# A quarter's even columns moved ahead of the softmax's exponential on ScalarE (graph attention with a sparse mask, then routed experts)

## The chip, the cores and the metric

One core of one Trainium2 chip. The metric is the device time of one launch in microseconds (us); lower is better. The kernel before takes 1185.52 us, the median of three runs (1185.07 to 1197.87).

## What is computed

```python
# x: 8192 x 256 f32; adj: 8192 x 8192 int32, about 1 in 2048 entries is 1, the others 0
h  = layernorm(x);  Wh = h @ W
e  = (Wh @ a1)[:, None] + (Wh @ a2)[None, :];  e = where(e > 0, e, 0.2 * e)
e  = where(adj > 0, e, -9e15)
x  = x + elu(softmax(e, axis=1) @ Wh)
h  = layernorm(x);  idx = argmax(h @ router_w.T + router_b)        # one of 32 experts
x  = x + relu(relu(h @ W1[idx] + b1[idx]) @ W2[idx] + b2[idx])
```

The mask `adj` is 268 MB, and reading it is most of the traffic. A row has about four neighbours, so the attention works on lists of neighbours and not on the full matrix.

## The kernel before

The 8192 rows are 64 strips of 128 rows. The program is written engine by engine, each engine with its own queue of instructions in the order of the code, and with counting semaphores between them. It has three stages: a table of `Wh` rows is built (eight groups of eight strips), then come the rounds, one step `u` for each strip, and then the experts work through blocks of tokens. The change lies in the rounds. A step handles several strips at once:

- **ScalarE** (`step` under `@block.scalar`) turns the mask of strip u+5 from int32 into fp8 bytes. A strip has four quarters of 2048 columns. The function `signs` (L711) writes one quarter with two instructions: the even columns (L717, ACT.Identity, out `sg`) and the odd columns (L719, ACT.Sign, out `sg`). The second one counts the semaphore `a_sg`. In a step the order is: `attention_sum` (L733, out `hh`), `count_tail` (L756, L758), quarter 0, `transposes2` (L744), quarter 1, `softmax_exp` (L749, out `pr` and `den`), `elu_exp` (L738, out `ex`), quarter 2, quarter 3.
- **SyncE** (queue SPq) loads the mask in halves of 2 MB (L427, `raw_all<-in_adj`). There are three half buffers. A load waits at L426 for `a_sg`, that is until ScalarE has finished the half that lies in its buffer. So each step issues two loads: one behind quarter 1 (here called load A) and one behind quarter 3 (load B).
- **TensorE** folds the bytes of a strip into words (`fold`, L1512 and L1514, out `psF`), and computes the weighted sum of the gathered rows (L1577, L1579), the tail's small products (L1546 to L1569) and fillers (L1503) that keep it busy.
- **VectorE** finds the neighbours in the words (L891 to L957), and does the softmax's scores (L1086 to L1106), the elu and the second normalisation (L1128 to L1158), and the place of each token with its expert (L1163 to L1196). It has by far the most instructions in a step, and works through them strictly in order.
- **GpSimd** issues the indirect DMAs on a queue of its own: at first the scatter of strip u-2 (L633, `regions<-x,posu`), then six gathers for strip u+1 (L611, `G_all<-wh_table,idx`): one for each of the first five neighbours, and a sixth, the tail gather, for all the neighbours beyond them, packed into slots.

Two of VectorE's instructions wait for those DMAs: L1086 (`slot_s`) for all six gathers of the strip, and L1140 (`x<-el,x_sb`) for the scatter that reads its buffer `x1`, of which there are two.

The rounds have 64 full steps, of which 59 read the mask ahead; most of these run in a loop whose body is two steps on most engines and six on ScalarE and SyncE.

Of the kernel before, what the change touches and what calls it, by code (L numbers as in the profile page):

```python
# [27 lines left out]
TINY = 1.0e-20  # L28
# [8 lines left out]
def gat_moe(nc, x, adj, gW, ga, rw, rb, W1, b1, W2, b2, out, table, region):  # L37
    f32, i32, u32 = mybir.dt.float32, mybir.dt.int32, mybir.dt.uint32
    bf16, f8 = mybir.dt.bfloat16, mybir.dt.float8e4
    ALU, ACT, AX = mybir.AluOpType, mybir.ActivationFunctionType, mybir.AxisListType  # L40
# [4 lines left out]
    LAG = NG // 2  # L45
# [15 lines left out]
    with ctx:  # L61
        def sb(name, shape, dt=f32):
            return ctx.enter_context(nc.sbuf_tensor(name, shape, dt))
# [4 lines left out]
        def sem(name):  # L68
            return ctx.enter_context(nc.semaphore(name))
# [22 lines left out]
        minus_half = sb("minus_half", [P, GROUP])  # L92
        minus_tiny = sb("minus_tiny", [P, 1])
# [35 lines left out]
        sign_of = [[[sg[i][:, q, :].bitcast(f8).rearrange("p (w b) -> p b w", b=2)[:, b, :] for b in range(2)] for q in range(Q)] for i in range(2)]  # L129
        raw_of = [[[raw[n][k].rearrange("p (w b) -> p b w", b=2)[:, b, :] for b in range(2)] for k in range(2)] for n in range(THIRDS)]  # L130
# [129 lines left out]
        a_sg = sem("a_sg")  # L260
# [104 lines left out]
        def half_place(strip, h):  # L365


            turn, rest = strip
            n = 2 * rest + h
            return n % THIRDS, turn * 2 + n // THIRDS  # L370
# [320 lines left out]
        def _(act):  # L691
# [16 lines left out]
                act.nop(nofuse=True)  # L708
                act.activation(xT[r % 2][:, :, :].rearrange("p h n -> p (h n)"), psXn[r % 2][:, 0:D], ACT.Copy).then_inc(a_xT, 1)  # L709

            def signs(t, par, q, strip):  # L711

                b, count = half_place(strip, q // 2)
                act.wait_ge(raw_in[b], count * 16 + 16)
                act.wait_ge(pe_fold, t * 2 + q // 2 + 1)
                act.nop(nofuse=True)
                act.activation(sign_of[par][q][0], raw_of[b][q % 2][0], ACT.Identity, bias=minus_tiny[:, 0:1], scale=TINY,  # L717
                               saturate=False)
                act.activation(sign_of[par][q][1], raw_of[b][q % 2][1], ACT.Sign, bias=minus_half[:, 0:1],  # L719
                               saturate=False).then_inc(a_sg, 1)  # L720

            def group(g, par, i, behind, ahead):
                for r in range(GROUP):
                    transposes(g * GROUP + r, r)
                    if r % 4 == 2:
                        signs(i, i % 2, 2 * par + r // 4, divmod(i, THIRDS))
            groups(act, group)

            def attention_sum(w, par):

                act.wait_ge(pe_o, w + 3)
                act.wait_ge(v_post, w * VP + VP + 2)
                act.activation(hh[:, :], psO[par][:, 0:D], ACT.Copy, scale=rden[par][:, 0:1]).then_inc(a_h, 1)  # L733

            def elu_exp(w):

                act.wait_ge(v_post, w * VP + 2 * VP + 1)
                act.activation(ex[:, :], um[:, :], ACT.Exp).then_inc(a_ex, 1)  # L738

            def transposes2(w):  # L740

                act.wait_ge(pe_t2, w + 1)
                act.wait_ge(pe_lg, w + 1)
                act.activation(xT2[:, :, :].rearrange("p h n -> p (h n)"), psT[:, 0:D], ACT.Copy).then_inc(a_x2, 1)  # L744

            def softmax_exp(u):

                act.wait_ge(v_sm, u * VS + VS)
                act.activation(pr[:, :], ee[:, :], ACT.Exp, bias=nmx[:, 0:1], accum_out=den[:, 0:1]).then_inc(a_p, 1)  # L749

            def count_tail(u, par):

                act.wait_ge(pe_slot, u + 1)
                act.wait_ge(v_dec, u * VD + VD)
                with nc.allow_low_precision(reason="counts of at most 11 are exact"):
                    act.activation(tail_sign[par][:, :], keys[:, bass.ds(u, 1), KD:K].rearrange("p o k -> p (o k)"), ACT.Sign,  # L756
                                   accum_out=tails[:, bass.ds(u, 1)]).then_inc(a_tail, 1)
                act.activation(tail_row[par][:, 0:KT], keys[:, bass.ds(u, 1), KD:K].rearrange("p o k -> p (o k)"),  # L758
                               ACT.Copy).then_inc(a_tail, 1)
# [3 lines left out]
            for q in range(Q):  # L763
                signs(LAG, 0, q, divmod(LAG, THIRDS))

            def step(u, par, do, strip):
                if do.post:
                    attention_sum(u - 1, 1 - par)
                if do.prepare:
                    count_tail(u + 2, par)  # L770
                if do.ahead:
                    signs(u + LAG + 1, 1 - par, 0, strip)
                if do.place:
                    transposes2(u - 2)
                if do.ahead:
                    signs(u + LAG + 1, 1 - par, 1, strip)
                if do.attend:
                    softmax_exp(u)
                if do.post:
                    elu_exp(u - 1)  # L780
                if do.ahead:
                    signs(u + LAG + 1, 1 - par, 2, strip)
                    signs(u + LAG + 1, 1 - par, 3, strip)
            rounds_of_six(act, step)

            act.wait_ge(v_flag, 6)
# [944 lines left out]
```

## Time and profile before

| | |
|---|---|
| median of three runs | 1185.52 us (1185.07 to 1197.87) |
| the profiled execution: its own time, its span | 1188.4 us, 1186.6 us |
| busy over the span (page): VectorE, ScalarE, TensorE, GpSimd | 894.5, 795.4, 900.9, 656.9 us |
| the rounds that this text counts in, from the scatter at 207.70 us to that at 935.58 us | 54 steps, 727.88 us |
| moved over the span | 357.33 MB, mean 301 GB/s |

The span is the time from the first to the last instruction. "Busy" counts the instructions of an engine that ran; a wait is shown as the idle time ahead of an instruction, with what ended it. For DMAs the profile tells when the instruction that issues one ran, and how long after it the data had landed.

### The profile page before, as it was taken

The page shows a single profiled execution, that of the slowest core. Times are in us where ns is not written, and L with a number is a line of the kernel's source. Part 1 is how long each engine was busy: PE and PEld are TensorE (multiplying, and loading weights), DVE is VectorE, ACT ScalarE, POOL GpSimd, SP SyncE. Part 2 cuts the span into 40 slices and gives each one's busy share as a digit, 9 for nine tenths or more (in the row PEclk, how much of TensorE's full clock was granted, in tenths as well). Part 3 has the DMA queues.
Part 4 walks back from the last instruction along what each step waited for, and adds up shares of the span by engine and source line. Part 5 has one row for each costly group of instructions (what it writes and reads, how often), then busy time and mean ns, then how long its engine had stood idle before and what let it go on. Part 6 is the DMA issues. An engine that isn't in the chain of part 4 may idle for free.

```text
span 1186.6 us, 25008 instructions
## 1 busy us (share of the span) xinstructions
PE 900.9 (76%) x4388; PEld 560.6 (47%) x4389; DVE 894.5 (75%) x4327; ACT 795.4 (67%) x1339; POOL 656.9 (55%) x700
## 2 busy tenths in 40 slices
PE   2777728788878888688887878878888875558995
PEld 1545515444444444354454444445445444446774
DVE  5788727688888878788888878878888876555563
ACT  0444549688887878688788877878878831136663
POOL 3555545556656655555565556655566556326664
PEclk9999959899999989899999999989999986679998
DMA  6677788899999999899999989998999995035651
GB/s 227 219 270 266 295 335 345 318 376 377 376 371 368 362 349 365 330 341 381 363 381 349 368 323 371 366 361 336 374 381 383 341 251 129 29 105 162 173 170 60
DMA packets 84715, 357.33 MB, mean 301 GB/s; under 512 B 26006, under 2 KB 52591, under 8 KB 68289
## 3 DMA queue, kind: packets, MB, share of 16 engines
q1 hardware_dynamic: 56226, 296.78, 67.7%
q0 software_dynamic: 27712, 60.06, 14.7%
q8 instruction: 12, 0.20, 0.1%
q14 instruction: 29, 0.24, 0.1%
q10 hardware_dynamic: 736, 0.05, 0.0%
HBM read 343.67 MB, written 32.05 MB: 317 GB/s over the span
## 4 chain that ended last, share of the span: by engine, by line
DVE 29%; DMA 23%; issue 22%; PE 13%; POOL 7%; DVEq 2%; ACT 2%; POOLq 0%; ACTq 0%
DMA regions<-x,posu 13%; DMA G_all<-wh_table,idx 7%; POOL G_all L611 4%; PE psO L1704 2%; DVE top_word L891 2%; PE psW L1494 2%; PE psO L1577 2%; POOL out_x L673 2%; DVE xn L1158 1%; DVE begun L1058 1%; DVE lidx L1173 1%; PE psO L1503 1%; DVE oh L1181 1%; DVE xn L985 1%; DVE el L1132 1%
## 5 line engine op out<-in xcount | busy, mean ns | idle before, releaser
L611 POOL DMA_INDIRECT G_all<-wh_table,idx x384 | 398.7, 1038 | 136.4 <-issue 128.7
L717 ACT ACTIVATE sg<-raw_all,minus_tiny 128x1024 fp8e4<-128x1024 int32 x256 | 311.8, 1218 | 0.1
L719 ACT ACTIVATE sg<-raw_all,minus_half 128x1024 fp8e4<-128x1024 int32 x256 | 311.1, 1215 | 0.0
L1503 PE MATMUL psO<-word_no,share 128*128 128x512 bf16 x885 | 244.0, 411 | 0.0
L633 POOL DMA_INDIRECT regions<-x,posu x64 | 67.4, 1053 | 213.9 <-DVE idx L1050 115.7
L1577 PE MATMUL psO<-G_all,diag 128*128 128x256 f32 x640 | 163.2, 405 | 22.9 <-DVE diag L1115 22.9
L1577 PEld LDWEIGHTS psO<-G_all,diag 128*128 128x128 f32 x640 | 124.3, 201 | 64.9 <-issue 48.4
L1512 PE MATMUL psF<-sg,fold_w 128*128 128x512 bf16 x512 | 136.0, 389 | 7.3 <-DVE top_word L891 2.7
L1503 PEld LDWEIGHTS psO<-word_no,share 128*128 128x128 bf16 x885 | 93.6, 111 | 92.9 <-issue 26.8
L749 ACT ACTIVATE pr<-ee,nmx 128x16 f32<-128x16 f32 x64 | 19.7, 307 | 146.3 <-DVE nmx L1106 146.3
L673 POOL DMA_INDIRECT out_x<-raw_all,tok x81 | 78.9, 974 | 56.6 <-issue 29.9
L891 DVE MAX8 top_word<-psF 128x8 f32<-128x256 f32 x256 | 103.0, 425 | 6.7 <-PE psF L1514 0.5
L1494 PE MATMUL psW<-w_aug,xT 128*128 128x258 f32 x256 | 69.5, 395 | 13.8 <-ACT xT L709 13.8
L583 POOL TENSOR_TENSOR xn_sum<-xn_sum,xn 128x256 f32<-128x256 f32 x64 | 47.5, 742 | 40.7 <-DVE xn L985 39.8
L1512 PEld LDWEIGHTS psF<-sg,fold_w 128*128 128x128 bf16 x512 | 47.1, 108 | 43.8 <-issue 13.4
L1704 PE MATMUL psO<-x_sb,hT 128*128 x162 | 56.0, 428 | 8.9 <-ACT hT L825 3.7
L1563 PE MATMUL psW<-slot_s,to_row 128*128 128x11 f32 x128 | 22.3, 248 | 49.3 <-DVE slot_s L1086 49.1
L627 POOL TENSOR_TENSOR x<-ve,minus_half 128x1 f32<-128x1 f32 x64 | 36.8, 576 | 35.6 <-DVE x L1154 34.7
L1563 PEld LDWEIGHTS psW<-slot_s,to_row 128*128 128x128 f32 x128 | 22.8, 204 | 69.8 <-issue 68.7
L1494 PEld LDWEIGHTS psW<-w_aug,xT 128*128 128x128 f32 x256 | 44.8, 195 | 22.7 <-issue 18.9
L817 ACT ACTIVATE w_b<-x_sb 128x129 f32 x84 | 26.3, 313 | 43.0 <-ACT hT L825 30.2
L1086 DVE TENSOR_SCALAR slot_s<-slot_col,G_all 128x11 f32<-128x11 f32 x64 | 16.6, 260 | 47.9 <-DMA G_all<-wh_table,idx 46.9
(217 smaller groups left out, 1837.5 us busy)
## 6 DMA issues: line engine op xcount, KB each, us to landing
raw_all<-in_adj SPq DMA_DIRECT2D x128, 2048.0 KB, 10.0
raw_all<-regions SPq DMA_DIRECT2D x84, 130.0 KB, 2.2
wh_table<-G_all POOLq DMA_DIRECT2D x8, 1040.0 KB, 10.0
x_sb<-in_x SPq DMA_DIRECT2D x8, 1024.0 KB, 5.7
G_all<-wh_table,idx POOLq DMA_INDIRECT x384, 6.1
regions<-pad_row SPq DMA_DIRECT2D x32, 130.0 KB
x_sb<-in_L_ffn_W SPq DMA_DIRECT2D x4, 512.0 KB
x_sb<-in_L_ffn_W SPq DMA_DIRECT2D x8, 256.0 KB
```

The costliest lines, as they stand in the source:

```text
L583: pool.tensor_tensor(xn_sum[:, :], xn_sum[:, :], xn[r % 2][:, :], ALU.add).then_inc(pl_sum, 1)
L611: pool.indirect_dma_start(out=G[par][:, k, :], out_offset=None, in_=table[:, :], in_offset=bass.IndirectOffsetOnAxis(ap=idx[par][:, k:k + ...
L633: pool.indirect_dma_start(out=region[:, :], out_offset=bass.IndirectOffsetOnAxis(ap=posu[par][:, 0:1], axis=0), in_=x1[par][:, :], in_offs ...
L673: pool.indirect_dma_start(out=out[:, :], out_offset=bass.IndirectOffsetOnAxis(ap=tok[r % STORES][:, 0:1], axis=0), in_=yb[r % STORES][:, : ...
L717: act.activation(sign_of[par][q][0], raw_of[b][q % 2][0], ACT.Identity, bias=minus_tiny[:, 0:1], scale=TINY, saturate=False)
L719: act.activation(sign_of[par][q][1], raw_of[b][q % 2][1], ACT.Sign, bias=minus_half[:, 0:1], saturate=False).then_inc(a_sg, 1)
L891: v.max(top_word[:, q, :], psF[q // 2][:, q % 2 * WORDS:(q % 2 + 1) * WORDS]).then_inc(v_top, 1)
L1494: mm = pe.matmul(psW[r % 2][:, 0:D + 2], xT[r % 2][:, h, :], w_aug[:, h, :], start=(h == 0), stop=(h == DH - 1))
L1503: pe.matmul(psO[par][:, :], share[:, :], word_no[:, 0:2, :].rearrange("p q w -> p (q w)"), start=True, stop=True)
L1512: pe.matmul(words, fold_w[:, j, :], sg[par][:, 2 * h:2 * h + 2, j * WORDS:(j + 1) * WORDS], start=(j == 0), stop=False)
L1577: pe.matmul(psO[par][:, 0:D], diag[:, k, :], G[par][:, k, 0:D], start=(k == 0), stop=False)
L1704: pe.matmul(psO[r % 2][:, 0:D], hT[r % 2][:, :], w2_sb[:, bass.ds(e, 1), :].rearrange("p o n -> p (o n)"), start=True, stop=True).then_inc ...
```

## The change

`signs` gets an argument that says which of the two byte columns it writes. In the step, quarter 2 is split: its even columns are written ahead of `softmax_exp`, its odd columns where the whole quarter was, behind `elu_exp`. Everything else stays.

```diff
-            def signs(t, par, q, strip):
+            def signs(t, par, q, strip, bytes=range(2)):
 
                 b, count = half_place(strip, q // 2)
                 act.wait_ge(raw_in[b], count * 16 + 16)
                 act.wait_ge(pe_fold, t * 2 + q // 2 + 1)
                 act.nop(nofuse=True)
-                act.activation(sign_of[par][q][0], raw_of[b][q % 2][0], ACT.Identity, bias=minus_tiny[:, 0:1], scale=TINY,
-                               saturate=False)
-                act.activation(sign_of[par][q][1], raw_of[b][q % 2][1], ACT.Sign, bias=minus_half[:, 0:1],
-                               saturate=False).then_inc(a_sg, 1)
+                if 0 in bytes:
+                    act.activation(sign_of[par][q][0], raw_of[b][q % 2][0], ACT.Identity, bias=minus_tiny[:, 0:1], scale=TINY,
+                                   saturate=False)
+                if 1 in bytes:
+                    act.activation(sign_of[par][q][1], raw_of[b][q % 2][1], ACT.Sign, bias=minus_half[:, 0:1],
+                                   saturate=False).then_inc(a_sg, 1)
...
                 if do.ahead:
                     signs(u + LAG + 1, 1 - par, 1, strip)
+                    signs(u + LAG + 1, 1 - par, 2, strip, range(1))
                 if do.attend:
                     softmax_exp(u)
                 if do.post:
                     elu_exp(u - 1)
                 if do.ahead:
-                    signs(u + LAG + 1, 1 - par, 2, strip)
+                    signs(u + LAG + 1, 1 - par, 2, strip, range(1, 2))
                     signs(u + LAG + 1, 1 - par, 3, strip)
```

ScalarE's queue in one step of the rounds, before, from the second instruction of quarter 1 to the first of the next step (in the names, `pr` is the softmax's exponential and `ex` the elu's):

```order
L719 ACTIVATE sg<-raw_all,minus_half 128x1024
L749 ACTIVATE pr,den<-ee,nmx 128x16
L738 ACTIVATE ex<-um 128x256
L717 ACTIVATE sg<-raw_all,minus_tiny 128x1024
L719 ACTIVATE sg<-raw_all,minus_half 128x1024
L717 ACTIVATE sg<-raw_all,minus_tiny 128x1024
L719 ACTIVATE sg<-raw_all,minus_half 128x1024
L733 ACTIVATE hh<-psO,rden 128x256
```

And after:

```order
L721 ACTIVATE sg<-raw_all,minus_half 128x1024
L718 ACTIVATE sg<-raw_all,minus_tiny 128x1024
L751 ACTIVATE pr,den<-ee,nmx 128x16
L740 ACTIVATE ex<-um 128x256
L721 ACTIVATE sg<-raw_all,minus_half 128x1024
L718 ACTIVATE sg<-raw_all,minus_tiny 128x1024
L721 ACTIVATE sg<-raw_all,minus_half 128x1024
L735 ACTIVATE hh<-psO,rden 128x256
```

One L717 (in the new file L718) has gone from behind `ex` to ahead of `pr`; the count of instructions is the same, and no other engine's order changes.

## Rows read from the trace of the kernel before

**Rows 1.** Rounds: window, us; busy PE, PEld, DVE, ACT, POOL; clock, DMA share, GB/s
```profile
207.70:935.58 727.88, 593.00 (x2864) 344.24 (x2862) 608.31 (x3132) 582.49 (x865) 423.44 (x432) 0.96 0.95 361
```

**Rows 2.** Waits of VectorE, 207 to 936 us: total, times, longest
```profile
DVE slot_s L1086 <- DMA G_all<-wh_table,idx: 23.3, 9, 4.7
DVE x L1140 <- DMA regions<-x,posu: 20.6, 23, 1.6
```

**Rows 3.** Timeline of GpSimd, two steps without such waits: start, duration [idle before]
```profile
884.64 1.06 POOL L633 DMA_INDIRECT regions<-x,posu  x1 [3.20 <-DVE idx L1050]
...
892.61 1.01 POOL L611 DMA_INDIRECT G_all<-wh_table,idx  x1 [0.30 <-DVE x L1154]
...
897.14 1.05 POOL L633 DMA_INDIRECT regions<-x,posu  x1 [2.90 <-DVE posu L1196]
...
910.11 1.06 POOL L633 DMA_INDIRECT regions<-x,posu  x1 [3.21 <-DVE idx L1050]
```

**Rows 4.** Timeline of ScalarE in two neighbouring steps
```profile
604.44 0.31 ACT L749 ACTIVATE pr<-ee,nmx 128x16 f32<-128x16 f32 x1 [1.98 <-DVE nmx L1106]
...
614.25 1.20 ACT L719 ACTIVATE sg<-raw_all,minus_half 128x1024 fp8e4<-128x1024 int32 x1
616.82 0.31 ACT L749 ACTIVATE pr<-ee,nmx 128x16 f32<-128x16 f32 x1 [1.37 <-DVE nmx L1106]
...
617.93 1.23 ACT L717 ACTIVATE sg<-raw_all,minus_tiny 128x1024 fp8e4<-128x1024 int32 x1
619.05 1.23 ACT L719 ACTIVATE sg<-raw_all,minus_half 128x1024 fp8e4<-128x1024 int32 x1
```

**Rows 5.** Source view of L749, 208 to 936 us: ScalarE's idle time before it
```profile
  DVE nmx L1106: 111.5, 54
```

**Rows 6.** Timeline of SyncE's loads (x2: from the first's start to the second's end)
```profile
602.67 7.98 SPq L427 DMA_DIRECT2D raw_all<-in_adj  x2
...
615.67 0.33 SPq L427 DMA_DIRECT2D raw_all<-in_adj  x1
...
622.75 7.00 SPq L427 DMA_DIRECT2D raw_all<-in_adj  x2
```

**Rows 7.** Timeline of VectorE: the instruction that needs the gathers, in two steps
```profile
613.96 0.23 DVE L1086 TENSOR_SCALAR slot_s<-slot_col,G_all 128x11 f32<-128x11 f32 x1
...
897.87 0.30 DVE L1086 TENSOR_SCALAR slot_s<-slot_col,G_all 128x11 f32<-128x11 f32 x1
```

**Rows 8.** Source view of L611, windows 608.9:609.2 and 621.7:622 (one tail gather each)
```profile
DMA to landing us min/median/max: 3.9/3.9/3.9
...
DMA to landing us min/median/max: 4.9/4.9/4.9
```

**Rows 9.** Timeline of SyncE: four other stretches with loads
```profile
181.21 6.18 SPq L427 DMA_DIRECT2D raw_all<-in_adj  x2
...
192.16 5.69 SPq L427 DMA_DIRECT2D raw_all<-in_adj  x2
...
216.18 7.32 SPq L427 DMA_DIRECT2D raw_all<-in_adj  x2
...
785.60 6.72 SPq L427 DMA_DIRECT2D raw_all<-in_adj  x2
```

**Rows 10.** L611, windows 187.6:189.7, 197.3:200.3, 216.1:216.4, 785.8:786.1 (the last two tail gathers)
```profile
L611 POOL DMA_INDIRECT G_all<-wh_table,idx x2: 1001/1256/1511, 187.7 to 189.5; - x2
DMA to landing us min/median/max: 6.3/6.7/7.2
...
L611 POOL DMA_INDIRECT G_all<-wh_table,idx x3: 1006/1027/1215, 197.4 to 200.1; - x3
DMA to landing us min/median/max: 7.6/7.7/8.3
...
DMA to landing us min/median/max: 9.9/9.9/9.9
...
DMA to landing us min/median/max: 8.7/8.7/8.7
```

## The prediction

> **What bounds the kernel now.** I read the busy table of the rounds first [rows 1]: of 727.88 us VectorE is busy 608, ScalarE 582, TensorE 593, and the DMA engines stand at a share of 0.95 with 361 GB/s. No compute engine is full, the DMA engines nearly are. The window holds 54 steps (as many exponentials in rows 5), so one takes 13.48 us, a pair 26.96.
>
> Then the waits of VectorE, which has 58 instructions a step and takes them strictly in order [rows 2]: 23.3 us for gathers ahead of `slot_s` (9 times, up to 4.7) and 20.6 us for the scatter ahead of L1140 (23 times). Together 43.9 us. Neither ScalarE nor TensorE takes more than a trace of VectorE's time. The scatters show what a pair costs without those waits: 910.11 - 884.64 = 25.47 us [rows 3]. Against 26.96 that is 1.49 more a pair, for 27 pairs 40 us, which agrees with the waits. So the step is VectorE's own queue (12.7 us) plus what it waits for small DMAs, and these wait because 4 MB of mask stream through the same 16 DMA engines in each step.
>
> Third, the timeline of ScalarE [rows 4]: it idles ahead of the softmax's exponential for 1.98 us in one step and 1.37 in the next, and that is so throughout: 111.5 us over 54 steps, 2.06 each [rows 5]. This idle time costs nothing in itself, since VectorE's `nmx` ends it.
>
> **The change, part by part.** *The moved instruction.* An L717 advances ScalarE's queue by 1.12 us (619.05 - 617.93) and is moved into the idle time. It can start where quarter 1 ends, at about 614.25 + 1.20 = 615.45, and lasts to some 616.65; the exponential starts at 616.82. So it fits with 0.2 us to spare in the tighter of two neighbouring steps and with 0.8 in the other [rows 4]. Cost on the exponential: nothing; bound above, 1.12 us in a step without idle time; the mean of 2.06 says that there are few. It adds a wait for the second half of the strip (load A of the step before) and for TensorE's fold, now ahead of the exponential, with `pr` and everything behind it queued. Load A is issued when quarter 1 ends and would be needed when quarter 1 ends again, one whole step later, 12.5 us or more. None of the `sg` instructions of rows 4 waited for a load. Cost nothing again, and that cover is one step long; if it were gone, each us that a load is late would be one of the step.
>
> *What comes earlier.* Behind `elu_exp` three instructions stand where four stood, so quarter 3 ends 1.12 us earlier, and `a_sg` lets SyncE issue load B 1.12 us earlier. ScalarE's next work (`hh`, `tail_sign`) waits for TensorE and VectorE soon anyway, so load A moves by 0 to 0.5 us. VectorE waits for nothing of this, so ScalarE's gain as such is worth 0.
>
> *What load B meets.* This is the term that decides. GpSimd's six gathers do not move: they follow the scatter. In one step the tail gather starts at about 609.0 and load B at 602.67 + 7.98 - 0.33 = 610.32, 1.3 us later; in the next the gather at 621.7 and load B at 622.75, one us later [rows 6, 8]. These two land 3.9 and 4.9 us after their start [rows 8]. VectorE needs them 5.0 us after it (613.96 - 608.96) in the one kind of step and 5.26 (897.87 - 892.61) in the other, when nothing else is late [rows 3, 7]. The slack is thus 0.4 to 1.1 us. After the change load B is issued 0.2 us behind the tail gather in the first kind and 0.1 ahead of it in the second.
>
> The trace has gathers that a load precedes or meets. Load at 187.06 (181.21 + 6.18 - 0.33): gathers at 187.7 and 189.5 land in 7.2 and 6.3 us. Load at 197.52: gathers from 197.4 to 200.1 in 7.6 to 8.3. Load at 216.18 and tail gather at 216.2: 9.9 us. Load at 785.60, tail gather at 785.9: 8.7 [rows 9, 10]. The mean of these seven (6.3, 7.2, 7.6, 7.7, 8.3, 8.7, 9.9) is 7.96. The last two stand at the very distance that the change makes, and VectorE's longest wait, 4.7 us [rows 2], is about what the 9.9 us leave (9.9 - 5.26 = 4.6). The ends are 6.3 and 9.9. I take the mean, since in the first two stretches the rounds were only starting, and in the last two GpSimd itself ran late in its step. The wait at `slot_s` is then 7.96 - 5.26 = 2.7 us; ends 1.04 and 4.64.
>
> It does not come in every step. A wait of w delays the exponential, hence load B, by w, while that step's own gathers have already been issued; the load is then 1 us or more behind the tail gather and this one lands in time. So every second step. A pair takes 25.47 + 2.7 = 28.2 us, with the scatter's waits gone: behind a late `slot_s` VectorE reaches L1140 late, and load B landing 1.1 us sooner frees the scatter in the other. Against 26.96 that is +1.2, for 27 pairs +33 us. Ends: 26.5 us and -12 us; 30.1 us and +85 us. Below the lower end only VectorE's waits are left to gain.
>
> The Trainium skill (page "DMA: Bandwidth & Descriptors", section "Queues, rings and completion order") says that each DMA engine alternates between the rings for which it has work, and changes only after a whole packet, typically some 9 to 17 descriptors; and that a completion is written only after all earlier writes of that DMA engine, of whatever queue. By that rule a gather behind a load waits for a large part of the load's share, and lands about when the load does. The trace agrees in kind (9.9 and 8.7 us, against 3.9 and 4.9).
>
> **Sum.** The profiled execution took 1188.4 us, its span 1186.6, so 1.8 us lie around it. 1188.4 + 33 = 1221; the median of the runs shown is 2.9 us lower, at 1185.5, so 1185.5 + 33 = 1219 us.
>
> **Rivals.** *A, faster: the scatter gains and the tail gather doesn't lose.* Load B lands 1.1 us sooner, so the scatter ahead of L1140 meets less of it, and the 20.6 us go [rows 2]. For it: in 23 of 54 steps that wait is there, at most 1.6 us, about what the load moves by. If `slot_s` goes on costing its 23.3, or a little more, that gives -15 to -20, some 1168 us. Against it [rows 9, 10]: no gather beside or behind a load's issue landed under 6.3 us. *B, no difference:* the two DMA effects cancel (w near 1.5 gives 26.97 a pair, exactly the pair of now), or VectorE's own queue sets all. 1185.5 us. For it: the DMA engines move the same bytes in both, and nobody waits for ScalarE. *C, much slower: the tail gather always lands with load B.* Then w is 4.64, a pair 30.1, +85 us, 1271. It decides from the point where load B's issue comes less than about 0.3 us behind the tail gather's in all steps. For it the two tail gathers of rows 10, 8.7 and 9.9; against it the lighter traffic that a longer pair brings, which lets a load land sooner. This is what the rule of the Trainium skill cited above (same page and section) gives if it holds in every such step. *D, the change fills nothing:* the exponential is late by the moved instruction. It costs at most 1.12 us a step, +60, 1246. Against it the idle times [rows 4, 5].
>
> **Chances.** The forecast (w between 1.9 and 4, 1196 to 1253 us) 0.40; C 0.13; D 0.02; B 0.20; A 0.25. A measurement of this kernel tells about 1% from no change. Faster by over 1%: 0.25; within 1%: 0.20; slower by over 1%: 0.55. For 8 in 10 the range takes in A's value at the low end and C's at the high end: 1168 to 1271.
>
> **What would show it.** Right: `slot_s` L1086 waits for `G_all` in some 25 of 54 steps, 2 to 4 us each, over 60 us in total; L1140's wait for the scatter falls under 10 us; the tail gathers before those waits land in 7 us or more; load B is issued within 0.3 us of the tail gather in the steps of 12.5 us; ScalarE's idle time ahead of `pr` alternates between about 0.5 and 3 us. Wrong: a pair of 26 us or less, with L1140 and `slot_s` both under their 20.6 and 23.3 us; then an early load does not hold up a gather, and its landing hangs on something else, as on GpSimd being late. Wrong in another way if load B is not issued earlier at all, because ScalarE waits for `um` or for the mask.

## The result, and the profile after

The changed kernel takes 1208.81 us, the median of four runs (1204.37 to 1212.42), against 1185.39 (1185.07 to 1197.87): a ratio of 1.0227, 95% interval 1.0169 to 1.0286. It is slower by 1.7 to 2.9%, as forecast (1219). The profiled execution took 1208.17 us, its span 1206.4; the one of before took 1188.4 and 1186.6, 3 us above its median. So the two traces have 19.8 us to explain.

The first view is the window that answers to [rows 1]: the same 54 steps of the rounds, now from the scatter at 210.39 us to that at 952.01 us. The columns are those of [rows 1].

```profile
210.39:952.01 741.62, 585.68 (x2810) 347.50 (x2862) 607.26 (x3132) 588.12 (x865) 424.41 (x433) 0.96 0.93 354
```

VectorE has its 3132 instructions and 607 us of work as before; ScalarE its 865. Only the time around them grew: 741.62 against 727.88, or 13.7 us. The rest lies outside the window: 2.7 us ahead of it (210.39 - 207.70) and 3.4 behind it (1206.4 - 952.01 against 1186.6 - 935.58; there the waits at `slot_s` went from 3.7 to 6.3 us). 2.7 + 13.7 + 3.4 = 19.8.

The waits of VectorE in that window, which answer to [rows 2]:

```profile
DVE slot_s L1089 <- DMA G_all<-wh_table,idx: 59.3, 27, 5.1
DVE idx L1053 <- issue: 13.2, 27, 0.6
DVE xn L1161 <- POOL x L627: 0.3, 1, 0.3
```

L1089 is the old L1086. It waits 27 times in 54 steps, 2.2 us each, where it waited 9 times for 23.3 us together. The wait of 20.6 us for the scatter is gone from the list altogether. So one wait took the place of the other, and more: 59.3 - 23.3 - 20.6 = +15.4 us, near the 13.7 by which the window grew.

Here are two neighbouring steps. First ScalarE, as in [rows 4]; L718 is now the even half of a quarter and L721 the odd one:

```profile
612.60 1.19 ACT L721 ACTIVATE sg<-raw_all,minus_half 128x1024 fp8e4<-128x1024 int32 x1
613.69 1.20 ACT L718 ACTIVATE sg<-raw_all,minus_tiny 128x1024 fp8e4<-128x1024 int32 x1
615.54 0.31 ACT L751 ACTIVATE pr<-ee,nmx 128x16 f32<-128x16 f32 x1 [0.65 <-DVE nmx L1109]
...
616.28 0.42 ACT L740 ACTIVATE ex<-um 128x256 f32<-128x256 f32 x1 [0.34 <-DVE um L1131]
...
618.84 1.22 ACT L721 ACTIVATE sg<-raw_all,minus_half 128x1024 fp8e4<-128x1024 int32 x1
620.67 0.47 ACT L735 ACTIVATE hh<-psO,rden 128x256 f32<-128x256 f32 x1 [0.60 <-PE psO L1582]
```

The moved instruction (613.69) sits in the idle time, and 0.65 us of that are left; `pr` is not late. Quarter 3 ends at 620.06 (618.84 + 1.22), one instruction earlier than it would behind the old order. What that frees is idle time again, ahead of `hh`. Now the issues, SyncE's loads (an issue of x2 spans both) and GpSimd's scatters (L633) and tail gathers:

```profile
614.01 6.62 SPq L427 DMA_DIRECT2D raw_all<-in_adj  x2
...
626.76 8.19 SPq L427 DMA_DIRECT2D raw_all<-in_adj  x2
```

```profile
611.91 1.05 POOL L633 DMA_INDIRECT regions<-x,posu  x1 [3.63 <-DVE posu L1199]
...
620.07 1.01 POOL L611 DMA_INDIRECT G_all<-wh_table,idx  x1 [0.30 <-issue]
...
624.88 1.06 POOL L633 DMA_INDIRECT regions<-x,posu  x1 [3.20 <-DVE idx L1053]
...
633.08 1.02 POOL L611 DMA_INDIRECT G_all<-wh_table,idx  x1 [0.31 <-issue]
```

And VectorE's instruction that needs the gathers:

```profile
627.11 0.23 DVE L1089 TENSOR_SCALAR slot_s<-slot_col,G_all 128x11 f32<-128x11 f32 x1 [1.97 <-DMA G_all<-wh_table,idx]
...
639.75 0.30 DVE L1089 TENSOR_SCALAR slot_s<-slot_col,G_all 128x11 f32<-128x11 f32 x1
...
653.95 0.41 DVE L1089 TENSOR_SCALAR slot_s<-slot_col,G_all 128x11 f32<-128x11 f32 x1 [1.71 <-DMA G_all<-wh_table,idx]
```

Load B goes out at 614.01 + 6.62 - 0.33 = 620.30 (0.33 is the length of one issue), 0.2 us behind the tail gather at 620.07. VectorE gets that gather's data 7.0 us after its start and has waited 1.97 us. The wait pushes the next exponential and with it the next load B to 626.76 + 8.19 - 0.33 = 634.62, 1.5 us behind the tail gather at 633.08; there is no wait at 639.75. In the step after, it is back. Over the middle of the rounds (300 to 700 us, 29 tail gathers) load B stands either 0.1 ahead to 0.3 us behind the tail gather, or 1.5 to 2.7 behind (5.6 once), about half and half; before, it stood 1.0 or 1.35 behind in most steps.

### The profile page after: what moved, and what is told of

Same layout as the page of the kernel before. It is cut to its first block, busy times and chain, and to the rows that moved or that the text cites. A ratio compares the mean times of both kernels' runs of the same rounds, so it can differ in the third digit from the quotient of the medians.

```text
span 1206.4 us, 25000 instructions
## 1 busy us (share of the span) xinstructions
PE 896.2 (74%) x4321; PEld 567.2 (47%) x4389; DVE 893.5 (74%) x4327; ACT 801.1 (66%) x1339; POOL 657.4 (54%) x700
## 4 chain that ended last, share of the span: by engine, by line
DVE 26%; issue 23%; DMA 22%; PE 13%; POOL 9%; ACT 3%; DVEq 2%; POOLq 0%; ACTq 0%; another core or an unknown queue 0%
DMA G_all<-wh_table,idx 17%; POOL G_all L611 7%; PE psO L1707 3%; DMA regions<-x,posu 2%; PE psO L1580 2%; DVE top_word L894 2%; PE psW L1497 2%; DVE el L1135 1%; POOL out_x L673 1%; PE psL L1696 1%; DVE xn L988 1%; ACT sg L721 1%; ACT sg L718 1%; DMA out_x<-raw_all,tok 1%; DVE xn L1161 1%
## 5 line engine op out<-in xcount | busy, mean ns | idle before, releaser
L611 POOL DMA_INDIRECT G_all<-wh_table,idx x384 | 399.4, 1040 | 136.9 <-issue 127.5
L718 ACT ACTIVATE sg<-raw_all,minus_tiny 128x1024 fp8e4<-128x1024 int32 x256 | 311.8, 1218 | 1.9 <-DMA raw_all<-in_adj 1.8
L721 ACT ACTIVATE sg<-raw_all,minus_half 128x1024 fp8e4<-128x1024 int32 x256 | 311.2, 1216 | 0.0
L1506 PE MATMUL psO<-word_no,share 128*128 128x512 bf16 x827 | 229.6, 410 | 3.2 <-issue 0.2
L633 POOL DMA_INDIRECT regions<-x,posu x64 | 67.5, 1054 | 215.4 <-DVE idx L1053 117.9
L1580 PEld LDWEIGHTS psO<-G_all,diag 128*128 128x128 f32 x640 | 129.0, 207 | 60.9 <-issue 43.2
L1506 PEld LDWEIGHTS psO<-word_no,share 128*128 128x128 bf16 x885 | 92.5, 109 | 87.1 <-issue 17.1
L735 ACT ACTIVATE hh<-psO,rden 128x256 f32<-128x256 f32 x64 | 30.4, 475 | 77.6 <-PE psO L1582 77.6
L1089 DVE TENSOR_SCALAR slot_s<-slot_col,G_all 128x11 f32<-128x11 f32 x64 | 16.3, 255 | 84.1 <-DMA G_all<-wh_table,idx 83.6
L1515 PEld LDWEIGHTS psF<-sg,fold_w 128*128 128x128 bf16 x512 | 47.2, 108 | 44.8 <-issue 13.8
```

What stands on the lines that cost most here:

```text
L611: pool.indirect_dma_start(out=G[par][:, k, :], out_offset=None, in_=table[:, :], in_offset=bass.IndirectOffsetOnAxis(ap=idx[par][:, k:k + ...
L633: pool.indirect_dma_start(out=region[:, :], out_offset=bass.IndirectOffsetOnAxis(ap=posu[par][:, 0:1], axis=0), in_=x1[par][:, :], in_offs ...
L1506: pe.matmul(psO[par][:, :], share[:, :], word_no[:, 0:2, :].rearrange("p q w -> p (q w)"), start=True, stop=True)
L1515: pe.matmul(words, fold_w[:, j, :], sg[par][:, 2 * h:2 * h + 2, j * WORDS:(j + 1) * WORDS], start=(j == 0), stop=False)
L1580: pe.matmul(psO[par][:, 0:D], diag[:, k, :], G[par][:, k, 0:D], start=(k == 0), stop=False)
```

## The experiments

Each ratio is against the kernel before, timed beside the run. "Gathers" is VectorE's total wait for gathers and "scatter" that for the scatter, both between 207 and 936 us of the profiled execution. That execution can be some 0.7% off the median of its kernel, so its waits go with its own time and not with the ratio. The code shown leaves out the `nop` behind each wait and the argument `late`, which is set for the loads in the rounds' steps.

### Load B late again, the new order kept

```diff
...
+                if late and h == 0:
+                    sp.wait_ge(a_tail, 2 * t - 7)
...
```

SyncE waits for one count more ahead of load B; nothing else differs from the changed kernel.

> The changed kernel, but SyncE's load B waits also for ScalarE's tail_sign behind quarter 3, so it is issued about 1 us later, where it was before the change; ScalarE's order stays the changed one. Theory 1 (an early load B holds up the tail gather): the waits at slot_s fall from over 80 us to 20-30 us, the scatter's waits return to some 20 us, 1180 to 1192 us. Rival (the new order on ScalarE costs by itself, by the added wait ahead of the exponential or by where the bytes come): it stays at 1203 to 1212 us, slot_s over 60 us.

Ratio 0.9997 (0.9961 to 1.0034), 1182.45 us. Load B now stands 1.67 us behind the tail gather (median of 30). VectorE's waits:

```profile
DVE x L1146 <- DMA regions<-x,posu: 26.0, 29, 2.6
DVE idx L1056 <- issue: 13.2, 27, 0.6
DVE slot_s L1092 <- DMA G_all<-wh_table,idx: 1.4, 4, 0.5
```

One wait on SyncE's queue, which does no work, takes back the whole 2%. So the new order on ScalarE costs nothing in itself that these runs can tell: its cost is the moment of load B. The gathers fell further than expected (1.4 us for 20 to 30), as this wait puts load B a little later than it was before the change, and the profiled execution (1173.99 us) was the fastest of ten.

### The same delay on the kernel before

> The kernel before, with the same added wait ahead of load B: issued about 1 us later than before, some 2 us behind the tail gather. Theory 1: the rare long landings of the tail gather (9 to 11 us) go, slot_s waits under 10 us; the scatter may wait longer since the load lands later (20 to 45 us), so 1165 to 1195 us. Rival: 1185 +- 4 us, slot_s as before at 23 us in the rounds.

Ratio 0.9966 (0.9934 to 0.9998), 1179.74 us; load B 1.9 us behind the tail gather.

```profile
DVE x L1143 <- DMA regions<-x,posu: 26.0, 36, 1.9
...
DVE slot_s L1089 <- DMA G_all<-wh_table,idx: 6.6, 4, 3.2
```

The gathers' waits went from 23.3 to 6.6 us as expected, the scatter's rose to 26.0. The gain is a third of a per cent and hardly clear of the measurement. Against the run above only the order on ScalarE differs, and the two intervals overlap.

### Load B much later

```diff
...
+                if late and h == 0:
+                    sp.wait_ge(a_sg, t * Q + 1)
...
```

> The changed kernel, load B waits also for quarter 0 of the next strip: some 3.5 us later than in the changed kernel. Theory 1: slot_s waits under 10 us, as the tail gather has landed when the load starts; but the load is then used less than 10 us after its issue, or the scatter meets more of it, so waits of ScalarE for the mask or of L1140 for the scatter come up: 1180 to 1215 us. Rival (order by itself): 1205 us or more with slot_s still over 60 us.

Ratio 1.0324 (1.0286 to 1.0362), 1221.36 us, a little above the range given, with load B 5.1 us behind the tail gather. No wait for gathers is in the list; it begins with

```profile
DVE x L1146 <- DMA regions<-x,posu: 72.3, 52, 2.6
```

ScalarE never waited for the mask in the rounds. Both theories allowed a slow result here, but with different waits, and the gathers' are gone. The load has an enemy on either side: too early it meets the tail gather, too late the scatter. One caution: the tail gather itself takes 5.4 us here (median of 26 landings), more than the 5.0 us at which VectorE asked for it before. That is not seen as a wait, as VectorE, held up by the scatter, mostly comes to `slot_s` only 6 us or more after that gather's start.

### Load B between

```diff
...
+                if late and h == 0:
+                    sp.wait_ge(a_h, t - 4)
...
```

> Dose between the changed kernel and the first run: load B waits for hh (ScalarE's instruction right behind quarter 3, itself waiting for TensorE), which puts it 0.4 to 0.9 us later than in the changed kernel. Theory 1: the waits at slot_s lie between 59 us (changed kernel) and 1.4 us (the run with about 1 us), say 5 to 35, and the scatter's between 0 and 26; 1180 to 1200 us. Rival (any wait on SyncE's queue would do): as the first run.

Ratio 0.9956 (0.9912 to 1.0000), 1180.51 us. `hh` itself waits for TensorE, so load B stands 1.3 us behind the tail gather, later than I had meant.

```profile
DVE x L1146 <- DMA regions<-x,posu: 16.6, 23, 2.8
DVE slot_s L1092 <- DMA G_all<-wh_table,idx: 13.8, 10, 3.4
```

These runs and the two kernels give a curve, all with two buffers and the tail gather last (the median distance is taken between 300 and 700 us):

| load B behind the tail gather (median), us | order on ScalarE | gathers, us | scatter, us | profiled execution, us | ratio of the medians |
|---|---|---|---|---|---|
| 0.3 (alternating -0.1..0.3 and 1.5..2.7) | new | 59.3 | 0 | 1208.17 | 1.0227 |
| 1.3 | old | 23.3 | 20.6 | 1188.4 | 1 |
| 1.3 | new | 13.8 | 16.6 | 1176.39 | 0.9956 |
| 1.7 | new | 1.4 | 26.0 | 1173.99 | 0.9997 |
| 1.9 | old | 6.6 | 26.0 | 1177.82 | 0.9966 |
| 5.1 | new | 0 | 72.3 | 1220.96 | 1.0324 |

At like distance both orders cost alike to within half a per cent, and the bottom is flat between 1.3 and 1.9 us. The two kinds of wait account for nearly all of the rest: taken off the profiled time they leave 1144.5 to 1148.9 us in all six rows, while the waits themselves go from 27.4 to 72.3 us.

### The tail gather first

```diff
-                gather(par, KD, GATHERS, gat)
+                gather(par, KD, GATHERS, gat_t)
...
-                    gather(1 - par, 0, KD, gat)
                     gather_tail(u + 1, 1 - par)
+                    gather(1 - par, 0, KD, gat)
...
-                v.wait_ge(gat[par], i16)
+                v.wait_ge(gat_t[par], i16)
...
+                v.wait_ge(gat[par], half_up(u, par) * KD)
```

`slot_s` needs only the tail gather; the other five are needed by the softmax's first instruction, 2.1 us later. With the new order:

> The changed kernel, GpSimd issues the tail gather first of the six and with a semaphore of its own; slot_s waits for that alone, the softmax's first instruction (about 2 us later) for the other five. Load B as early as in the changed kernel. Theory 1: slot_s does not wait for gathers any more; the fifth gather is now the last one, beside load B, but needed 2.1 us later, so of the waits of 2 us nearly nothing is left; the scatter's waits stay away as in the changed kernel: a pair of 25.5 to 26.2 us, 1145 to 1170 us. Rival (order by itself): 1200 us or more.

Ratio 1.0070 (1.0046 to 1.0094), 1192.42 us: better than the changed kernel, and not what I expected.

```profile
DVE sc L1102 <- DMA G_all<-wh_table,idx: 36.8, 29, 3.5
...
DVE x L1145 <- DMA regions<-x,posu: 1.0, 4, 0.3
```

`slot_s` no longer waits, but the softmax does in 29 of the steps, 1.27 us on average, though it comes 2.1 us later. In these 29 steps the gather that is now last is there about 2.1 + 1.27 - 2.2 = 1.2 us later after its start than the tail gather was. I had assumed the two alike. In ten more steps load B stood as near and nothing waited. The number of rows hardly explains it: with one entry in 2048, I estimate 48 rows of a strip with a fifth neighbour and 53 neighbours beyond the fifth. Why it takes longer stays open.

The same on the old order:

> Old order on ScalarE, tail gather first with a semaphore of its own. Load B is issued 1 us or more behind the last gather, which now has 2.1 us more until it is needed. Theory 1: the gathers' waits fall from 23.3 us to under 12 (what is left of the landings of 9 to 11 us), the scatter's waits stay at 20 to 28 us or grow by what is gained: 1172 to 1184 us. Rival (the gathers' waits are not bound to which gather is the last): 1185 us.

Ratio 0.9904 (0.9869 to 0.9940), 1174.24 us.

```profile
DVE sc L1099 <- DMA G_all<-wh_table,idx: 20.0, 12, 3.6
DVE x L1142 <- DMA regions<-x,posu: 19.4, 25, 1.6
```

The time came as expected, the waits did not: 20.0 us for gathers and not under 12. This profiled execution (1181.37 us) was among the slower of its ten, so part of the gain is not in it.

The two steps together, with the new order and load B behind `hh`:

> Changed order, tail gather first, load B behind hh. With the last gather needed 2.1 us later and load B 0.4 to 0.9 us later than in the changed kernel, theory 1 has the gathers' waits fall from 36.8 us (the same with load B early) to 5 to 20 and the scatter's stay under 15: 1168 to 1184 us, better than both kernels. Rival (a fixed sum: what one DMA gains the other loses): 1185 to 1192 us.

Ratio 0.9880 (0.9830 to 0.9929), 1169.00 us: the lowest of all, 1.2% below the kernel before (0.7 to 1.7%), though its interval overlaps with that of the last run. The profiled execution was its fastest of seven (1161.32 us).

```profile
DVE x L1148 <- DMA regions<-x,posu: 17.0, 22, 1.6
DVE idx L1057 <- issue: 13.2, 27, 0.6
DVE sc L1105 <- DMA G_all<-wh_table,idx: 4.4, 3, 1.8
```

And with load B behind `tail_sign`:

> As the last, load B behind tail_sign, about 1 us later than in the changed kernel. Gathers' waits under 5 us, the scatter's 20 to 28 us as in the first run: 1176 to 1186 us.

Ratio 0.9899 (0.9854 to 0.9943), 1174.29 us; it can't be told from the last two. Gathers 4.3 us, scatter 30.6, a little more than expected.

### Three buffers for the scatter

If the scatter's waits and the gathers' are all that stands above VectorE's own queue, a third buffer `x1` (with one more for the places, `posu`) removes the first kind. It needs loop bodies of six steps on VectorE and GpSimd, so a control has those alone:

```diff
...
-            rounds(pool, step)
+            rounds_of_six(pool, step)
...
-            rounds(v, step)
+            rounds_of_six(v, step)
```

> Control for the next three: the kernel before with VectorE's and GpSimd's loop bodies six steps long instead of two, nothing else. The loop's turn costs VectorE 0.5 us ahead of the first instruction of every second step (13.2 us in the rounds of the kernel before); that should fall to about 4.5 us. Where that idle time covers the scatter's landing, it comes back as a wait at L1140. Expected 1176 to 1187 us; a wait on fetched code could make it slower.

Ratio 1.0406 (1.0311 to 1.0501), 1243.18 us. The control alone is 4% slower, which I had given as a mere possibility.

```profile
DVE idx L1050 <- issue: 50.2, 9, 7.0
DVE slot_s L1086 <- DMA G_all<-wh_table,idx: 32.2, 18, 5.1
DVE x L1140 <- DMA regions<-x,posu: 22.1, 18, 2.8
```

The turn of the loop now comes 9 times and costs 5.6 us each, for 27 times 0.49. Three more instructions of VectorE idle without a releaser, 12.4 us together, where the kernel before has 0.2. These two and the gathers' 8.9 us more add up to 58 of the 59 us between the two profiled spans. The page of the profile counts 97 packets on the queue for instructions where the kernel before has 29:

```profile
q14 instruction: 97, 0.79, 0.2%
```

The three-buffer kernels are read against this control only:

```diff
...
-        x1 = [sb(f"x1{i}", [P, ROW]) for i in range(2)]
+        x1 = [sb(f"x1{i}", [P, ROW]) for i in range(3)]
...
-                    scatter(u - 2, par)
+                    scatter(u - 2, par, (strip[1] + 2) % 3, sc_out)
...
-                    post_x1(w, 1 - par, x_rows(w), None if isinstance(w, int) and w < 2 else half_done(w, 1 - par))
+                    post_x1(w, strip[1], x_rows(w), None if isinstance(w, int) and w < 3 else strip[0] * 16 - 32)
```

> As the control, and three buffers x1 instead of two, so that VectorE waits for the scatter of three strips ago. If the rounds are VectorE's queue plus the waits for the scatter and for the tail gather, the waits at L1140 (20 to 26 us) go to zero and the time falls by 12 to 25 us against the control, unless the gained time comes back at slot_s: with shorter steps the DMA engines are fuller and load B still meets the tail gather within 1 us. 1155 to 1175 us. If the DMA engines' throughput bounds the rounds instead, it is within 5 us of the control and the waits move to slot_s.

1228.14 us (1224 to 1244), 15 less than the control (1235 to 1249), within the 12 to 25 expected of the difference; the absolute time was missed with the control's. The scatter's wait is gone, the gathers' the same:

```profile
DVE slot_s L1090 <- DMA G_all<-wh_table,idx: 31.7, 26, 6.3
```

With the new order:

> As the last, with the changed order on ScalarE. Theory 1 (an early load B holds up the tail gather): the waits at slot_s stay at some 2 us in every second step, 45 to 60 us together, since no scatter is involved; the time is 1190 to 1205 us, 20 us or more above the same kernel with the old order. Rival (the scatter's buffers are what the early load disturbs): the difference between the two orders goes.

1253.87 us (1245 to 1257), 25.7 more than the same with the old order (+2.1%, as large as the change's own effect). The difference came as expected, the absolute time did not; the waits are fewer and longer, 3.5 us in 17 steps:

```profile
DVE slot_s L1093 <- DMA G_all<-wh_table,idx: 59.2, 17, 6.5
```

No scatter waits in either, so what the early load costs does not go by way of the scatter's buffers.

Old order, load B behind the next quarter 0:

> Three buffers x1, old order on ScalarE, and load B issued only behind quarter 0 of the next strip, some 2.4 us later than before. Theory 1: the late load costs only at the scatter (as in the third run of the first set), which no longer matters, and leaves the tail gather free: both waits near zero, a pair of steps 25.5 us less the loop's turn, 1140 to 1155 us. If instead the load is now late for ScalarE (it is used about 11 us after its issue and lands in 10), waits of sg for the mask appear and it is 1155 to 1185 us.

1218.92 us, 24 less than the control, but the gathers' waits did not vanish: 43.7 us in 34 steps, more than the control's 32.2. Most of the 24 us is not a gain of the DMAs either: the loop's turns cost 32.1 us here and 50.2 in the control, for a reason that no run shows. The two loads are now issued 2.5 us apart, around the scatter, and the gathers follow right behind them:

```profile
607.65 2.82 SPq L431 DMA_DIRECT2D raw_all<-in_adj  x2
```

```profile
608.12 1.06 POOL L636 DMA_INDIRECT regions<-x,posu  x1 [3.64 <-DVE idx L1057]
```

I had counted only the distance of load B to the tail gather ahead of it, and not that a load too late is a load ahead of the next step's gathers. (That these two loads are what holds them up is argued from the timeline; this trace has no landings of the gathers. In the run with load B much later, where the two loads stand alike, the tail gather takes 5.4 us.)

## Why the prediction was right, and where it was off

**The moved instruction costs nothing.** Right in the window: 0.65 us of idle time are left ahead of `pr` in the step shown, and over the window ScalarE still idles there 87.1 us, where it was 111.5. In five of the 54 steps no idle time was left, yet VectorE waited for `pr` in none of them. Its bound, "there are few" steps without idle time, was true and not nothing. In two of the three steps ahead of the window VectorE waited for `pr`; in the kernel before, its waits of this kind came to 0.5 us in the whole run:

```profile
188.22 0.16 DVE L1114 RECIPROCAL rden<-den 128x1 f32<-128x1 f32 x1 [0.83 <-ACT pr L751]
...
200.82 0.16 DVE L1114 RECIPROCAL rden<-den 128x1 f32<-128x1 f32 x1 [1.11 <-ACT pr L751]
```

That is 1.9 us in the stretch that grew by 2.7: rival D, in two steps of 64. Other waits of VectorE moved both ways there (1.9 us less for gathers, 1.8 and 1.3 us more for two results of TensorE), so the 1.9 is not the whole account.

**Load B 1.12 us earlier, beside the tail gather.** Right to 0.1 us: forecast 0.2 behind and 0.1 ahead, measured 0.23 behind and 0.12 ahead, in the steps that no wait had shifted. The first run keeps the order, takes back the shift, and with it the loss.

**Every second step.** Right: 27 waits in 54 steps, with the load 1.5 us and more behind in the others (0.9 in one).

**The size of the wait.** This is the term that was mis-sized. I took 7.96 us for the landing, the mean of seven gathers [rows 10], and 2.7 us of wait. VectorE's waits end on average 7.3 us after the tail gather's start, and the wait is 2.2 us. A pair is 741.62 / 27 = 27.47 us and not 28.17; over 27 pairs that takes 19 us off the 33 forecast, so 14 in the window. Of the 19, 13.5 are the wait (2.2 for 2.7) and 5.4 the pair without waits, 25.27 us ((741.62 - 59.3) / 27) and not the 25.47 read off one pair. What lies around the window, for which I had counted nothing, added 6. The two landings of 8.7 and 9.9 pulled the mean up, and they came with a late GpSimd, as I had written; the other five (6.3 to 8.3) have a mean of 7.4. Waits of more than 3 us came twice in the window (5.1 and 4.3).

Better rows stood in every step of the kernel before, beside load A. The first gather starts 0.5 us ahead of load A and the second 0.8 us behind it; over the 52 steps from 240 to 930 us they land 7.4 and 7.5 us after their start (medians). In the step of [rows 8] (source view of L611, windows 602.2:602.4 and 603.6:603.8, with load A at 602.67):

```profile
DMA to landing us min/median/max: 7.5/7.5/7.5
...
DMA to landing us min/median/max: 7.3/7.3/7.3
```

A wait of 7.4 - 5.26 = 2.1 us would have come from them. They also bound what I said against rival A: the third to fifth gathers, 2.1 to 4.8 us behind load A, land in 6.4, 5.5 and 4.5 us, so a gather behind a load does not always take 6.3 us or more; those within 1 us of its issue mostly do.

**The scatter's waits go.** Right, 20.6 us to none. Rival A had that part right and lost on the gathers. Rival C (every landing as long as load B's) is out with its 4.6 us of wait: in 18 of the 27 steps the trace has load B's landing, 8.9 us after its issue on average, and the gather's data was there 1.6 us before it (0.2 to 3.4). The Trainium skill (page "DMA: Bandwidth & Descriptors", section "Queues, rings and completion order") says that a DMA engine drains a whole packet of one ring before it turns to the next, and that a completion comes only after the engine's earlier writes, of all its queues. The runs agree in direction, but the delay here is about 2 to 3 us (7.3 us against 5.0, the median landing of the tail gather before) and not the load's full time. Whether turn-taking between the rings or the order of completions makes it, no run here separates.

**What the sum rested on.** That the rounds are VectorE's queue plus two kinds of wait held in every run with the old loops: the profiled time less these waits is 1144.5 to 1148.9 us in the table, and 1140 to 1147 us in the four runs with the tail gather first. The three buffers agree with it for the scatter: 22.1 us of waits removed, 15 us gained, with executions from 1235 to 1249 us for the one kernel and from 1224 to 1244 us for the other.

## What to carry to other kernels

When an engine off the critical path gets faster, look at what its semaphore releases: here it released a 2 MB load 1.1 us earlier, and that cost 2%. Small DMAs with little slack want a gap of a known length to the large load that follows and to the one before; measure the time as a function of that distance with one cheap wait on the issuing queue, and give the small transfers slack first (own semaphore, the urgent one issued first). The version that does both runs at 0.988 of the kernel before. Whether its new order on ScalarE adds anything to the tail gather going first on the old order (0.990), the intervals don't tell.

## What the runs showed of the hardware

- A tail gather started within 0.3 us of a 2 MB load's issue is there 7.3 us after its start on average (27 waits of the changed kernel, one of them with the load 1.1 us ahead); started 1 us or more ahead of it, it is mostly there before VectorE asks, 5.0 to 5.3 us after its start (median 5.0 in the kernel before; 3.9 and 4.9 in [rows 8]).
- Among tail gathers that lead the load by 1.0 to 1.35 us a few still take long: in the kernel before three of 47 landed after 9.0, 10.7 and 11.0 us and cost 12.2 of the 23.3 us. Two of its nine waits (8.5 us) were gathers that the load met or preceded. With 1.7 and 1.9 us of lead all waits for gathers came to 1.4 and 6.6 us. What makes the rare long ones, no run shows.
- Loop bodies of six steps instead of two on VectorE and GpSimd made each turn of the loop cost VectorE 5.6 us instead of 0.5, with 97 instead of 29 packets on the instruction queue. Nine long turns cost 50.2 us, 27 short ones 13.2.
